# A new order of the same steps on five engines, in a kernel that pipelines two attention branches

## The reference, cut to what matters

```python
def reference(...):
    x = L0_attn_x
    xn = _layernorm(x, axis=-1)
    x = x + _L0_attn_ref(xn, ...) + _L0_ffn_ref(xn, ...)
    return x

# branch 1, "full": 16 heads of 8, attention along the rows n of each token block
scores = jnp.einsum('nqhd,nkhd->nhqk', Q, K) * scale
attn = jax.nn.softmax(scores, axis=-1)
out = jnp.einsum('nhql,nlhd->nqhd', attn, V)

# branch 2, "local": two layers one after the other; 8 heads of 64, windows of 64 tokens
def _layer(x, wqkv, qs, ksc, wo, lg, lb, w1, b1, w2, b2):
    h = shift_token(x)
    q, k, v = jnp.split(h @ wqkv, 3, axis=-1)          # to heads
    q = l2norm(q) * qs
    k = l2norm(k) * ksc
    q, k = rotary_xpos(q, k)
    x = x + local_attention(q, k, v) @ wo              # each window sees itself and the one before
    h = layernorm(shift_token(x)) * lg + lb
    a, g = jnp.split(h @ w1 + b1, 2, axis=-1)
    return x + (a * gelu(g)) @ w2 + b2
```

## Time and profile before

| | before |
|---|---|
| time, median of 3 runs (range) | 1640.23 us (1639.82 to 1640.68) |
| the profiled execution: its time, its span | 1646.02 us, 1644.0 us |
| busy: PE, DVE, ACT, POOL | 1440.7, 1402.0, 1438.2, 1338.4 us |
| instructions | 37326 |

### The profile page before, as it was taken

The page is one execution under the profiler, slowest core; times in us unless marked ns, Lnnn a source line. Parts: engine busy times, 40 slices in busy tenths (PEclk is TensorE's granted clock), DMA queues, the critical chain, the costliest instruction groups (busy, mean ns, idle before and its releaser), DMA issues.

```text
span 1644.0 us, 37326 instructions
## 1 busy us (share of the span) xinstructions
PE 1440.7 (88%) x13496; PEld 1008.8 (61%) x13496; DVE 1402.0 (85%) x2052; ACT 1438.2 (87%) x4432; POOL 1338.4 (81%) x713
## 2 busy tenths in 40 slices
PE   1657999999999999999999999999999999999775
PEld 1545666666666666666666666666666666666553
DVE  3969899999999899999999999999989999998251
ACT  0647999999999999999999999999999999999582
POOL 2848988899888888898888889888888899888250
PEclk9878999999999999999999999999999999999797
DMA  5112212132222212222221213222221222221110
GB/s 148 24 32 43 56 24 56 39 67 45 62 56 62 52 27 53 51 56 56 62 56 37 56 34 67 44 62 56 63 51 27 53 51 56 49 62 36 33 30 26
DMA packets 206849, 82.91 MB, mean 50 GB/s; under 512 B 143266, under 2 KB 185676, under 8 KB 206668
## 3 DMA queue, kind: packets, MB, share of 16 engines
q1 hardware_dynamic: 205372, 79.97, 22.5%
q10 hardware_dynamic: 1296, 0.56, 0.1%
HBM read 17.60 MB, written 8.39 MB: 16 GB/s over the span
## 4 chain that ended last, share of the span: by engine, by line
ACT 53%; PE 20%; issue 8%; DVE 8%; DMA 6%; POOL 4%; SPq 1%; ACTq 0%; POOLq 0%; DVEq 0%
ACT sb_pl L552 12%; ACT sb_pl L559 10%; ACT sb_pT L502 6%; ACT sb_sq L529 5%; DMA sb_hs<-sb_x 4%; ACT sb_gate L583 3%; PE banks L866 3%; ACT sb_v L502 3%; PE banks L771 2%; ACT L552 2%; ACT L583 2%; ACT sb_kT L502 2%; DVE sb_qk L699 2%; DVE sb_t L704 2%; PE banks L845 2%
## 5 line engine op out<-in xcount | busy, mean ns | idle before, releaser
L477 POOL TENSOR_TENSOR sb_qk<-sb_qk,sb_t 128x1024 f32<-128x1024 f32 x128 | 306.3, 2393 | 121.2 <-DVE sb_t L704 121.2
L483 POOL TENSOR_TENSOR sb_rn<-sb_rn,sb_half 128x16 f32<-128x16 f32 x128 | 374.5, 2926 | 10.7
L552 ACT ACTIVATE sb_pl<-banks,sb_nml 128x128 f32<-128x128 f32 x1024 | 368.1, 401 | 2.3 <-DVE sb_nml L715 1.8
L559 ACT ACTIVATE sb_pl<-sb_pl,sb_rl 128x128 f32<-128x128 f32 x1024 | 334.3, 451 | 11.2 <-DVE sb_rl L720 11.2
L472 POOL TENSOR_TENSOR sb_pr<-sb_qkvf 128x2048 f32<-128x2048 f32 x64 | 291.1, 4548 | 31.3 <-DVE sb_qkvf L662 28.7
L489 POOL TENSOR_TENSOR sb_qk<-sb_qk,sb_rn 128x1024 f32<-128x1024 f32 x128 | 243.8, 1904 | 16.6 <-POOL sb_rn L483 0.4
L552 ACT ACTIVATION_READ_ACCUMULATOR sb_pl<-banks,sb_nml 128x1 f32 x1024 | 247.2, 241 | 0.0
L715 DVE TENSOR_REDUCE sb_nml<-banks 128x4 f32<-128x512 f32 x256 | 167.3, 680 | 37.5 <-PE banks L845 37.5
L855 PE MATMUL banks<-sb_ident,sb_pl 128*128 128x128 f32 x1024 | 157.2, 282 | 38.8 <-ACT sb_pl L559 19.2
L771 PE MATMUL banks<-sb_wqh,sb_hh 128*128 128x512 f32 x384 | 171.9, 448 | 17.2 <-DVE sb_t L704 10.3
L699 DVE TENSOR_TENSOR sb_qk<-banks,sb_tab 128x1024 f32<-128x1024 f32 x128 | 155.2, 1212 | 34.8 <-ACT sb_sq L529 33.7
(11 more groups left out here) (116 smaller groups left out, 3412.9 us busy)
## 6 DMA issues: line engine op xcount, KB each, us to landing
sb_vs<-sb_v SPq DMA_DIRECT2D x224, 128.0 KB, 2.4
sb_xt<-x SPq DMA_DIRECT2D x16, 256.0 KB, 3.1
sb_hh<-sb_sh SPq DMA_DIRECT2D x32, 128.0 KB, 2.4
sb_hl<-sb_sl SPq DMA_DIRECT2D x32, 128.0 KB, 2.4
heads_scratch<-sb_ofs SPq DMA_DIRECT2D x64, 64.0 KB, 3.3
sb_hs<-sb_x SPq DMA_DIRECT2D x32, 128.0 KB, 2.3
sb_orow<-heads_scratch SPq DMA_DIRECT2D x16, 256.0 KB, 4.0
sb_ob<-x SPq DMA_DIRECT2D x16, 256.0 KB, 3.3
```

The costliest lines, as they stand in the source:

```text
L477: nc.gpsimd.tensor_tensor(qk[:, k, :], qk[:, k, :], t2[:], ALU.add).then_inc(s_add.sem, 1)
L483: nc.gpsimd.tensor_tensor(rn[:, k, :], rn[:, k, :], half[:, 0:1].to_broadcast([P, 16]), ALU.pow).then_inc(s_rn.sem, 1)
L552: last = nc.scalar.activation(pl[:, k, m, :], ps[:, m * P:(m + 1) * P], ACT.Exp, bias=nml[:, k, m:m + 1], accum_out=suml[:, k, m:m + 1])
L559: last = nc.scalar.activation(pl[:, k, m, :], pl[:, k, m, :], ACT.Copy, scale=rl[:, k, m:m + 1])
```

## The change

Only the table changes: the slots of every step, and the two edge terms. The kinds of steps, their engines, tiles, waits and counts stay. In slots, the last `down` of a unit moves from 107.54 to 126.94 behind its first `project_qk`, the units still 50 apart; the first unit is moved 1.13 slots later instead of 11.19, the last one 6.33 sooner instead of 17.85. Where the planner deals the PSUM banks it follows the new list.

```diff
@@ -34,7 +34,7 @@
 
 PERIOD = 50.0
 LAYER_AT = (0.0, 3 * PERIOD)
-FIRST_LATER, LAST_SOONER = 11.19, 17.85
+FIRST_LATER, LAST_SOONER = 1.13, 6.33
 
 
 def spaced(first, gap, n):
@@ -42,38 +42,38 @@
 
 
 UNIT_SLOTS = {
-    "shift_x": (-4.14,), "project_qk": (0.00, 10.79, 20.70, 33.41), "square": (2.72, 13.64, 27.89, 36.99),
-    "rope": (6.73, 19.01, 28.57, 42.34), "ssq": (5.68, 19.22, 31.99, 45.51), "rope_add": (11.54, 19.72, 32.94, 47.84),
-    "rnorm": (6.12, 24.26, 33.94, 50.27), "normed": (15.28, 25.55, 34.59, 52.56), "project_v": (15.24, 15.43, 32.25, 43.42),
-    "v_copy": (17.29, 20.80, 37.54, 43.91), "move_v": (28.13, 47.26, 62.01, 73.06), "qk_t": (18.80, 31.43, 42.47, 57.08),
-    "q_copy": (19.73, 35.06, 42.94, 57.96), "k_copy": (19.72, 33.01, 43.02, 58.48), "scores": (24.88, 35.57, 45.39, 59.97),
-    "row_max": (27.15, 27.46, 40.02, 41.55, 45.84, 46.80, 61.55, 62.32),
-    "exp": (28.39, 32.20, 41.96, 43.27, 52.64, 57.52, 62.47, 64.97),
-    "row_recip": (30.83, 34.94, 44.90, 46.06, 57.15, 58.98, 64.69, 68.97),
-    "scale": (32.88, 35.19, 50.04, 54.40, 59.46, 59.80, 69.09, 70.25),
-    "probs_t": (33.62, 39.26, 54.13, 56.62, 60.49, 66.18, 70.60, 71.08),
-    "p_copy": (36.15, 41.39, 55.63, 58.70, 64.76, 68.16, 70.68, 73.99), "values": (45.88, 62.78, 70.40, 75.26),
-    "o_copy": (50.43, 65.48, 71.13, 75.97), "out_local": (78.57,), "x2": (80.56,), "shift_x2": (81.66,), "center": (85.17,),
-    "center_sq": (85.72,), "variance": (88.56,), "veps": (89.12,), "rstd2": (93.25,), "spread": (94.82,),
-    "normed2": (95.42,), "high2": (97.48,), "low2": (99.04,), "up": (100.30, 103.17, 104.01),
-    "gelu": (103.25, 103.60, 105.06), "hid": (103.91, 104.55, 105.74), "down": (107.54,),
+    "shift_x": (-3.82,), "project_qk": (0.00, 14.11, 28.76, 38.54), "square": (6.11, 19.33, 31.74, 42.22),
+    "rope": (10.74, 25.21, 36.75, 46.03), "ssq": (13.97, 21.89, 42.12, 47.81), "rope_add": (16.33, 30.85, 43.48, 54.20),
+    "rnorm": (25.85, 29.42, 50.23, 57.09), "normed": (27.11, 36.02, 53.31, 57.43), "project_v": (31.85, 48.36, 54.05, 59.20),
+    "v_copy": (32.37, 50.15, 57.53, 59.48), "move_v": (45.36, 53.43, 78.65, 80.90), "qk_t": (27.43, 40.33, 55.01, 66.39),
+    "q_copy": (29.89, 43.15, 55.55, 67.09), "k_copy": (28.67, 43.54, 55.78, 67.23), "scores": (32.84, 43.61, 56.58, 73.25),
+    "row_max": (36.85, 37.33, 46.97, 46.99, 58.74, 59.95, 73.67, 75.62),
+    "exp": (39.37, 41.47, 47.53, 54.77, 59.95, 60.91, 75.58, 79.23),
+    "row_recip": (42.15, 45.74, 49.19, 58.72, 65.29, 65.31, 77.05, 85.28),
+    "scale": (44.51, 45.79, 56.16, 65.40, 72.54, 74.18, 78.54, 85.41),
+    "probs_t": (45.09, 52.98, 61.43, 72.72, 74.47, 80.19, 83.38, 87.28),
+    "p_copy": (47.04, 55.54, 62.54, 75.60, 78.30, 80.86, 86.05, 88.07), "values": (60.73, 81.17, 86.44, 88.63),
+    "o_copy": (64.22, 83.44, 89.58, 90.23), "out_local": (91.88,), "x2": (96.57,), "shift_x2": (98.83,), "center": (103.57,),
+    "center_sq": (105.11,), "variance": (105.60,), "veps": (106.19,), "rstd2": (111.36,), "spread": (111.48,),
+    "normed2": (112.58,), "high2": (114.09,), "low2": (114.68,), "up": (117.10, 118.01, 119.93),
+    "gelu": (118.57, 119.21, 120.28), "hid": (119.91, 121.01, 122.39), "down": (126.94,),
 }
 FIRST_SLOTS = {
-    "x1": (109.14,), "x1_split": (125.41,), "x1_low": (127.21,),
+    "x1": (130.12,), "x1_split": (137.04,), "x1_low": (138.02,),
 }
 SEQ_SLOTS = {
-    "load": (-96.62,), "stats": (-39.51,), "rstd1": (-33.75,), "norm": (-26.01,), "norm_t": (-24.65,), "x_split": (-20.76,),
-    "x_low": (-19.80,), "qkv_full": (-9.08, -3.29, 27.00, 46.62), "qkv_bias": (-8.02, 0.20, 29.85, 47.47),
-    "product": (-5.79, 4.84, 44.23, 68.77), "full_scores": (1.91, 22.30, 49.15, 73.78),
-    "full_exp": (8.65, 28.23, 57.72, 82.50), "full_values": (14.39, 36.74, 62.62, 87.60),
-    "heads": (36.77, 43.17, 72.34, 115.57), "heads_load": (158.53,), "attn_t": (164.12,), "o_t": (168.39,),
+    "load": (-102.13,), "stats": (-92.42,), "rstd1": (-86.04,), "norm": (-62.45,), "norm_t": (-13.79,), "x_split": (-13.58,),
+    "x_low": (-9.54,), "qkv_full": (-1.47, 13.39, 19.95, 63.22), "qkv_bias": (-0.97, 15.22, 23.22, 67.71),
+    "product": (11.75, 32.06, 65.96, 87.74), "full_scores": (18.51, 42.70, 68.08, 93.97),
+    "full_exp": (25.46, 46.96, 74.91, 96.10), "full_values": (30.42, 53.56, 79.32, 103.58),
+    "heads": (55.44, 67.92, 95.53, 144.92), "heads_load": (154.59,), "attn_t": (198.14,), "o_t": (202.60,),
 }
 PREP_SLOTS = {
-    "split_w3": (-480.06,), "split_q": (-92.09, -13.09), "tables": (-18.77, 60.23), "fold": (27.68,), "gain": (79.90,),
-    "split_up": (84.56,), "biases": (88.53,),
+    "split_w3": (-416.26,), "split_q": (-72.16, 6.84), "tables": (-1.30, 77.70), "fold": (31.15,), "gain": (40.71,),
+    "split_up": (63.00,), "biases": (106.84,),
 }
 LAST_SLOTS = {
-    "x_again": (120.48,), "result": (111.49,), "final": (119.41,), "add_x": (127.82,), "store": (187.93,),
+    "x_again": (131.81,), "result": (131.04,), "final": (145.47,), "add_x": (147.20,), "store": (198.98,),
 }
 
 
```

## The result

The changed kernel takes 1590.15 us (median of 4 runs, 1588.55 to 1592.92) where the kernel before took 1640.45 beside it: 0.969 of it, interval 0.966 to 0.972, so 3.1% faster. I forecast 1617, with 1592 to 1660 as the range. The direction was right; the gain was 50 us and not 23, just outside the range. The profiled execution took 1592.92 us with a span of 1590.9.

What follows compares the result with a forecast made beforehand. ACT's fixed work plus its idle time was taken to set the span; start -2.7, fill -4, middle -23 and end +6 gave about -23, so 1640.2 became 1617 us, range 1592 to 1660.

Steps and rivals of the forecast that it cites:

- The frame: Whole kernel: span is ACT's 1438.2 us of unchanged work plus 205.8 idle; a new order changes only the idle time.
- At `o_copy`: ACT's wait for `values`: 2.33 us of cover against 2.06 needed, so it goes; at worst half of 1.0 a unit stays.
- At `center_sq`: ACT's wait for `center`: 0.2 to 1.6 us stays in layer 0, none in layer 1; 0.4 a unit against 0.66.
- the two bounds behind this term: PE's time between `out_local` and `center` in layer 0 units: 6.8 us at most, 5.4 if the transposes overlap the rest.
- At `scale` and the first `probs_t`: Old 8.5 us wait goes; new ones of 0.5 us a unit at the seventh `scale`, 0.2 at the first `probs_t`.
- all waits go: Rival, middle units: the deeper pipeline gives every result more distance, -52 us there, -53 in all, 1587; chance 0.12.
- The start: Until the first `project_qk`: `stats` moves ahead of a split, -2.7 us if `norm` still hides the split.
- The fill: From first `project_qk` to unit (2, 0): idle time -4 us, bounds -10 and +5; unit (1, 0) starts near 106.
- the product's move: In the fill, a `product` of 4.52 us on POOL leaves unit (0, 0)'s chain, making `out_local` some 4.5 us earlier.
- The end: Behind the last `down` of (15, 0): less of (14, 1) left to keep ACT busy; +6 us, bounds 0 and +14.

Runs made afterwards that it cites:

- `o_copy` uncovered: Changed kernel with the last two `o_copy` of every unit put back directly behind the last `p_copy`: 1652.64 us, 1.005 of the kernel before.
- `center` unshifted: Kernel before, with `center` reading the residual itself instead of its copy shifted by one position, output not the reference's: 1624.58 us, 0.988.
- the early statistics alone: Changed kernel with the split of the first weights moved behind the statistics and the first wqkv split on VectorE: 1580.03 us, 0.962 of the kernel before.
- the product put back: Changed kernel with the third product of the first sequence back ahead of the last `rope_add` of unit (0, 0) on POOL: 1583.30 us, 0.964.
- the second split moved: Changed kernel with the second (layer 1) weight split moved from behind `qkv_bias` to ahead of `x_low` on VectorE: 1589.85 us, 0.967.
- the first split put back: Changed kernel with the first wqkv split put back ahead of the first statistics on VectorE: 1590.96 us, 0.968 of the kernel before.

## Why the prediction was off

**The frame** held: the span is ACT's work plus its idle time, and in the middle only ACT's waits matter. I took its busy time as constant. In the middle it fell by 6.9 us, from 1165.4 to 1158.5, with the same instructions. There were 65 waits and there are 15: each that went took 0.14 us of busy time along. Copies are issued 0.48 apart and last 0.60, so the last stretch of a step, which otherwise lies under the next one, is counted when nothing follows. That reading is argued, not tested, and the other orders follow it only roughly: busy 1164.8 us with 80 waits (`o_copy` uncovered), 1167.6 with 54 (`center` unshifted).

**At `o_copy`** the step was right: 2.33 us of cover against 2.06 forecast, 2.34 measured, no wait. The thin margin held. That this wait is worth its own size and not more was wrong: with the cover taken back, the kernel lost some 60 us.

**At `center_sq`** it was right and nearly the right size: `center` ends 11.5 us behind the start of `o_copy` (forecast 10.9 to 12.3), ACT fills 11.0 (10.7). Of the 7.4 us of wait 6.3 are in layer 0 units, 0.5 us each; over all units that is 0.28 and not 0.4. Of the two bounds behind this term the lower, 5.4 us between `out_local` and `center`, doesn't follow from its own prices (without the four transposing steps they leave 4.4); 5.9 were measured.

**At `scale` and the first `probs_t`** is the step that failed: "I take 0.5 a unit for this and 0.2 for the first `probs_t`". No such wait came, at either place. ACT's timeline at a seventh `scale`, and DVE's:

```profile
756.74 1.28 ACT L596 ACT_TABLE_LOAD   x1
758.03 0.37 ACT L596 ACTIVATE banks<-banks 128x256 f32<-128x256 f32 x1
758.31 0.36 ACT L552 ACTIVATE sb_pl<-banks,sb_nml 128x128 f32<-128x128 f32 x1
...
759.68 1.11 ACT L502 ACTIVATE sb_pT<-banks 128x512 f32<-128x512 f32 x2
760.64 1.31 ACT L559 ACTIVATE sb_pl<-sb_pl,sb_rl 128x128 f32<-128x128 f32 x4
```

```profile
756.15 0.69 DVE L715 TENSOR_REDUCE sb_nml<-banks 128x4 f32<-128x512 f32 x1
...
759.85 0.18 DVE L720 RECIPROCAL sb_rl<-sb_suml 128x4 f32<-128x4 f32 x1
```

I had DVE run `rope` and `row_max` after the `exp`. But the `exp` itself started 1.5 us after its `row_max` was ready, because ACT had a table load and `full_exp` first. DVE did its two steps while ACT got to the `exp` and through it, and the reciprocal was there 0.6 us before `scale` asked. A list of what stands in each queue doesn't say when the engine arrives there; I needed the absolute times on both.

In numbers, the middle: -23 forecast; 0.82 a unit less kept (1.1 against 0.28, and 0.7 of it at the step above, 18 us) is -21; busy time -7; together -51.

**Against "all waits go"** I argued that PE and DVE would be at 97% and be waited for. They are at 95.8 and 95.9%, and ACT waits 7.4 us for PE and not at all for DVE. (DVE's 1125.7 at 90 us a sequence would have been 96% and not 97.) PE's busy time fell from 1137.5 to 1119.1 us with the same matmuls, so the figure wasn't a fixed amount of work, and a share near one was no bound. That rival, 1587, had 0.12 and was the case that came, though part of its closeness is luck: the fill took 8 us more idle time than its term, the end 6 less, and ACT's busy time, which it held constant, fell by 7.6.

**The start**: -4.1 and not -2.7. The statistics came 2.95 us earlier (0.3 of it from earlier loads), and POOL's part behind them shrank by 1.1. But the place of the split, which I gave as the reason, is worth little: with the split back in front, POOL starts 3.2 us later (0.5 of it from later loads) and is 2.0 us faster.

**The fill** was wrong: -4 forecast, +3.6 measured in idle time. `out_local` of (0, 0) ended at 113.2 and not at 104.1, and unit (1, 0) started at 113.6, directly behind it, and not near 106. No gain of the product's move showed. The new places of DVE's splits and tables beside POOL's products stretched three steps of DVE by 4.2, 3.3 and 2.5 us (5.96, 4.26 and 3.68 us against 1.76, 0.96 and 1.22 alone); with the three out of POOL's way ACT's idle time in the fill was 53.0 against 57.1 with the early statistics alone, one profile each. My terms have no entry for DVE's part of the preparations. The rest is clock: `fold` ran at the lower one in both profiles of the changed kernel (idle time in the fill 58.8 and 61.3) and at the upper one with the product put back, the second split moved and the first split put back (56.1, 54.3 and 54.6, against 55.1 before the change). So, as far as these profiles show, the order of the fill was worth about nothing, and the +3.6 is partly chance.

**The end**: +6 forecast, -0.4 measured, and the last stretch alone varies by as much as the term (last section). I counted that (14, 1) would leave less work beside (15, 1), and behind the last `down` ACT was idle for 3.1 us more. But (15, 0)'s own stretch took up 11.4 us more of ACT's work (96.6 to 108.0) and lost 3.5 us of its 5.6 of idle time, which I had no term for, and the two cancel.

## What to carry over

When an engine does the same work in every order, add up its waits: in seven versions of this kernel, length less named waits stayed within 1%. The sum doesn't say which engine makes the time; an edit that moves steps of one engine alone does. A wait at the head of a queue can be covered by another unit's work, but look at what stands behind the late result in the other engines' queues: where those kept the old order, the wait walked to the next queue and grew. And small steps on the path of the start should run while nobody holds up their engine.
